# Two transformer layers with expert routing on one core: the passes of the last stage in another order, its row scatters in other groups, its last sums on two engines

## The chip, the core and the metric
One of the cores of a Trainium2 chip runs the whole program. The metric is the device time in microseconds (us); lower is better. The engines are TensorE (PE), VectorE (DVE), ScalarE (ACT), GpSimd (POOL) and SyncE (SP), which mostly issues DMAs. Each works through its own list of instructions in order and waits on semaphores.

## The reference
Input x is 2 x 512 x 256, float32. Four sublayers follow one another, each on the layernorm of x and added to x:
```
x = x + attn0(ln(x))   # delta rule over 512 steps, 16 heads of 16
x = x + ffn0(ln(x))    # 8 experts, top 2, and a shared expert
x = x + attn1(ln(x))   # 16 query heads of 128, 2 key/value heads, causal, softcap 30
x = x + ffn1(ln(x))    # 16 experts, top 6, hidden 176
# ffn1, T = 1024 tokens:
scores = softmax(h @ gate_w.T);  topk_w, topk_idx = top_k(scores, 6)
for e in range(16):
    out = (silu(h @ w_gate[e].T) * (h @ w_up[e].T)) @ w_down[e].T
    y = y + cw[:, e:e+1] * out
```
The change touches the end of attn1 and all of ffn1.

## The kernel before
**attn1** runs over 32 heads n (two batches of 16). Per head TensorE does scores, turns the output of the head before, the next head's queries, the projection of the head before, and the products of probabilities and values; ScalarE does tanh and exp, GpSimd the causal mask (L1138), VectorE the rotations and the normalising.

**ffn1** works on two halves of 512 tokens. For each half the router (`route_a`, `route_b1` to `b3`, VectorE) picks six experts a token, `places1` (TensorE) counts rows, `rows1_index` (VectorE) makes the indices, and GpSimd scatters each row with `send_rows` into a DRAM tensor `rows1`, ordered by expert in blocks of 64 rows: 24 indirect DMAs a half. For the first half (batch 0) this lies in heads 20 to 30: four scatters a head in heads 25 to 30. For the second half it lies in the loop over pairs.

**The loop over pairs** (L1387 TensorE, L1507 ScalarE, L1679 VectorE, L1142 GpSimd) has 64 turns J, 32 a half. A pair is two blocks of 64 rows with possibly two experts. Its steps:
- SP loads its 128 rows (`load_rows`, five buffers).
- turn (`pair_turn`, L657): two transposes of 128 x 128 on TensorE; ScalarE copies the result (`pair_x`).
- gate-up (`pair_gate_up`, L673): the two blocks use the 64-column halves of the array, each with its own expert's weights. The second block's weights are at a place that a register gives; ScalarE copies them to a fixed place first (`pair_copy_gu`, L716), VectorE does the same for down (`pair_copy_dn`, L725).
- silu (ScalarE, L741), mul (VectorE, L754).
- hidden (`pair_hidden`, L685): two transposes of 128 x 88; VectorE copies the result (`pair_h`, L760, here "h").
- down (`pair_down`, L699): 88 x 64 weights, again two halves; ScalarE copies (`pair_y`, L747) into one of 18 buffers, and GpSimd scatters that to DRAM (`send_back`, L781) into a tensor `ret` in token order.

All orders are written out by hand, with the step's number as the condition. In turn J TensorE does turn(J+2), gate-up(J+1), hidden(J), down(J-1), and VectorE mul(J+1), h(J), table copy(J) and then whatever else is set for that J. There is one bank of PSUM each for the results of turn, hidden and down, and two for gate-up. The extras on VectorE: first index back at 1, residual of the last head and layernorm at 2 to 4, the router of the second half at 6 to 11, its index at 12, tables at 13 to 16, and from turn 52 two weighted adds a turn for the first half.

When all of a half's returns have landed, SP loads six tensors of 512 KB (`load_back`, one for each of the six choices, four token tiles each), and VectorE adds tile by tile with the weight as a scalar (`add_back`, L790): 24 adds a half. Then the output is stored.

## Time and profile before
| | us |
|---|---|
| median of 3 runs | 867.38 (866.95 to 867.87) |
| the profiled execution | 867.91 |
| its span, first to last instruction | 866.1 |

| busy, share of the span | |
|---|---|
| TensorE matmul | 789.5 us, 91% |
| VectorE | 507.1 us, 59% |
| ScalarE | 400.1 us, 46% |
| GpSimd | 278.8 us, 32% |
| mean granted TensorE clock | 0.970 |

The profile follows one execution. A start is counted from the span's start. Matmuls are pipelined and their ends are modelled, so lengths are best read from one start to the next. The chain that ended last lies on TensorE for 62% of the span and on VectorE for 12%. The loop over pairs fills the time from 625 to 846 us.

### The profile page before, as it was taken

Reading aid. Unit: us, or ns where it says so; the run is one execution under the profiler, and the core shown is the slowest. Engines: PE = TensorE matmul, PEld = TensorE weight load, DVE = VectorE, ACT = ScalarE, POOL = GpSimd, SP = SyncE. Lnnn points to the kernel's source line nnn. Section 1 sums busy time; section 2 is a strip of 40 time slices with the busy share of each in tenths; the row PEclk is TensorE's granted clock in tenths of the full one; section 3 lists DMA queues with packets and bytes.
Section 4 is the critical chain, followed back from the end, with each engine's and each line's share of the span. In section 5 each row is a group of like instructions: output and inputs, shape, how many; then the busy total and the mean of one; then the engine's idle time right before and its main releaser. Section 6 shows DMA issues by size and latency. Waiting matters only on the chain.

```text
span 866.1 us, 15945 instructions
## 1 busy us (share of the span) xinstructions
PE 789.5 (91%) x5107; PEld 521.6 (60%) x5107; DVE 507.1 (59%) x1270; ACT 400.1 (46%) x856; POOL 278.8 (32%) x374
## 2 busy tenths in 40 slices
PE   5988799889979998999999999899899999999990
PEld 3566566676557785777777767667654444444440
DVE  5999876666512236756556655777534763443564
ACT  3987777555123333443233342232527454555540
POOL 3643744113500033111111111137602265554430
PEclk9998999999989999999999999999979999999995
DMA  4002770181253221044453533113232243537316
GB/s 140 2 1 37 244 257 2 35 238 51 80 165 109 86 67 56 19 142 134 134 159 122 171 92 78 53 50 101 90 68 68 62 126 116 135 117 245 101 46 212
DMA packets 103590, 91.22 MB, mean 105 GB/s; under 512 B 38104, under 2 KB 95448, under 8 KB 103512
## 3 DMA queue, kind: packets, MB, share of 16 engines
q1 hardware_dynamic: 93288, 67.92, 27.2%
q0 software_dynamic: 6912, 19.28, 6.4%
q10 hardware_dynamic: 3312, 3.02, 1.0%
q8 instruction: 45, 0.74, 0.4%
q14 instruction: 33, 0.27, 0.1%
HBM read 50.47 MB, written 38.67 MB: 103 GB/s over the span
## 4 chain that ended last, share of the span: by engine, by line
PE 62%; DVE 12%; issue 6%; POOL 5%; DMA 4%; ACT 3%; DVEq 0%; ACTq 0%; SPq 0%; POOLq 0%
PE bank L1383 8%; PE bank L1346 7%; PE bank L673 7%; PE bank L1240 6%; PE bank L1226 5%; PE bank L699 5%; PE bank L896 3%; PE bank L2166 3%; POOL rows L771 3%; PE bank L918 2%; PE bank L657 2%; PE bank L2123 2%; PE bank L2150 2%; DMA rows<-arena,sidx 2%; PE bank L685 2%
## 5 line engine op out<-in xcount | busy, mean ns | idle before, releaser
L1487 ACT ACTIVATE arena<-bank 128x512 f32<-128x512 f32 (+1 forms) x96 | 46.9, 525 | 147.5 <-PE bank L1346 147.4
L1138 POOL TENSOR_TENSOR arena<-arena,causal_t 128x256 f32<-128x256 f32 x64 | 45.1, 726 | 214.0 <-ACT arena L1492 214.0
L781 POOL DMA_INDIRECT ret<-arena,ridx x64 | 66.1, 1033 | 103.9 <-ACT arena L747 49.9
L673 PE MATMUL bank<-arena 128*64 (+1 forms) x512 | 91.0, 477 | 1.0 <-DVE arena L733 1.0
L1383 PEld LDWEIGHTS bank<-arena 128*128 128x128 f32 x640 | 76.6, 192 | 5.2 <-POOL arena L1138 2.7
L1383 PE MATMUL bank<-arena 128*128 128x129 f32 x640 | 77.5, 276 | 1.7 <-POOL arena L1138 1.7
L1346 PE MATMUL bank<-arena 128*128 128x512 f32 (+3 forms) x256 | 75.7, 440 | 1.4 <-DVE arena L1546 1.4
L699 PE MATMUL bank<-arena 88*64 (+1 forms) x512 | 69.8, 393 | 3.2 <-DVE arena L725 1.7
L754 DVE TENSOR_TENSOR arena<-arena,bank 128x176 f32<-128x176 f32 x64 | 21.6, 337 | 86.2 <-ACT arena L741 86.0
L1240 PE MATMUL bank<-arena 128*128 128x256 f32 x256 | 62.6, 389 | 1.5 <-DVE arena L1553 1.5
L1240 PEld LDWEIGHTS bank<-arena 128*128 128x128 f32 x256 | 49.4, 194 | 22.6 <-issue 12.1
L1226 PE MATMUL bank<-arena 128*128 128x512 f32 x128 | 60.5, 595 | 0.5 <-DVE arena L1544 0.5
L771 POOL DMA_INDIRECT rows<-arena,sidx x48 | 49.9, 1039 | 32.1 <-issue 11.9
L716 ACT COPY arena<-arena 128x704 f32 x64 | 49.7, 778 | 20.5 <-issue 17.1
L1346 PEld LDWEIGHTS bank<-arena 128*128 128x128 f32 x256 | 41.8, 193 | 27.3 <-issue 19.1
L747 ACT COPY arena<-bank 128x256 f32<-128x256 f32 x64 | 23.8, 372 | 69.9 <-PE bank L699 59.8
L673 PEld LDWEIGHTS bank<-arena 128*64 128x64 f32 x512 | 31.5, 137 | 31.8 <-issue 31.6
L1553 DVE COPY arena<-bank 128x256 f32<-128x256 f32 x64 | 24.1, 418 | 42.1 <-PE bank L1250 41.9
L699 PEld LDWEIGHTS bank<-arena 88*64 88x64 f32 x512 | 31.2, 136 | 25.0 <-issue 15.9
L1542 DVE TENSOR_TENSOR arena<-bank,arena 64x512 f32<-64x512 f32 x36 | 24.9, 693 | 35.8 <-PE bank L1226 30.1
L2166 PE MATMUL bank<-w,arena 128*128 128x128 f32 x248 | 35.5, 286 | 7.1 <-DVE w L2699 3.3
L1492 ACT ACTIVATE arena<-arena 128x1280 f32<-128x1280 f32 x32 | 40.6, 1270 | 1.0
(288 smaller groups left out, 1527.0 us busy)
## 6 DMA issues: line engine op xcount, KB each, us to landing
rows<-arena SPq DMA_DIRECT2D x16, 544.0 KB, 4.6
rows_in<-place SPq DMA_DIRECT2D x5, 1664.0 KB, 14.4
arena<-rows SPq DMA_DIRECT2D x64, 128.0 KB, 2.1
arena<-in_w_gu SPq DMA_DIRECT2D x24, 256.0 KB, 3.5
arena<-ret SPq DMA_DIRECT2D x12, 512.0 KB, 6.7
arena<-in_w_dn SPq DMA_DIRECT2D x24, 176.0 KB
arena<-in_wq SPq DMA_DIRECT2D x32, 128.0 KB, 3.9
arena<-in_wo SPq DMA_DIRECT2D x32, 128.0 KB, 2.0
```

Of the source, the lines that this page charges most:

```text
L673: mm = nc.tensor.matmul(p_gu[J % 2][u * HR:(u + 1) * HR, 0:2 * FE].rearrange("p (y n) -> p y n", y=2), pxT[:, J % 2, k, u * HR:(u + 1) * H ...
L699: mm = nc.tensor.matmul(p_y[u * HR:(u + 1) * HR, :], phT[0:HB, J % 2, q, u * HR:(u + 1) * HR], w[u][:, q, :], start=(q == 0), stop=(q == 1 ...
L716: nc.scalar.copy(wbg[:, J % 2, :], w1_gu[:, bass.ds(off, GU1)]).then_inc(s_wbg, 1)
L771: nc.gpsimd.indirect_dma_start(rows1[h], bass.IndirectOffsetOnAxis(ap=sidx1[:, h, i % K1, i // K1:i // K1 + 1], axis=0), xa[h][:, i // K1, ...
L781: nc.gpsimd.indirect_dma_start(ret[h], bass.IndirectOffsetOnAxis(ap=ridx[:, h, j:j + 1], axis=0), py[J % NY], None).then_inc(s_ret, 16)
L1138: nc.gpsimd.tensor_tensor(blocks, blocks, causal_t[:].unsqueeze(1).to_broadcast([P, 2, P]), ALU.mult).then_inc(s_p, 1)
L1226: mm = nc.tensor.matmul(b_q[:], wq[:, n % 2, k, :], xnT2[:, k, b * SEQ:(b + 1) * SEQ], start=(k == 0), stop=(k == KD - 1))
L1240: mm = nc.tensor.matmul(b_y[t // 2][:, (t % 2) * DIM:(t % 2 + 1) * DIM], oT[:, t * P:(t + 1) * P], wo[:, n % 2, :], start=first and t % 2 ...
L1346: mm = nc.tensor.matmul(b_s[sbank][:, o:o + w], kT[:, grp, kt * P:(kt + 1) * P], qr[:, kt * P:SEQ], start=True, stop=True, skip_group_chec ...
L1383: mm = nc.tensor.matmul(b_o[pair][:, t * (DH + 1):(t + 1) * (DH + 1)], pr[:, o:o + P], v[:, grp, kt, :], start=(kt == 0), stop=(kt == qb))
L1487: nc.scalar.activation(th[:, sbank * 512:sbank * 512 + w], b_s[sbank][:, 0:w], ACT.Tanh, scale=SCALE / SOFTCAP).then_inc(s_th, 1)
L2166: mm = nc.tensor.matmul(sacc[h][:, j * P:(j + 1) * P], kq[:, u, hq * P:(hq + 1) * P], ub[s][:, hq, :], start=False, stop=True, skip_group_ ...
```

## The change
TensorE's order in turn J becomes turn(J+2), hidden(J-1), gate-up(J+1), down(J-1); the first gate-up comes behind head 31's values. VectorE's order becomes h(J-1), mul(J+1), table copy(J). The extras get other turns: first index back 4 (from 1), both stats 2, normalise 3, router 5, 6, 8, 10, index 11, tables 13, 15, 16, 17, three adds a turn in 54 to 61. The first half's scatters go in groups of five in heads 25 to 29, the second half's in four groups of six. The second half's returns are loaded from two queues (SP and ScalarE); token tiles 0 and 1 are added on VectorE, tiles 2 and 3 by TensorE with diagonal matrices of the weights, which VectorE writes in turns 40 to 45, and one add from PSUM. Scatter groups wait for the group before, as they did. On TensorE the extras of turn J stand behind hidden(J-1) and ahead of gate-up(J+1); before they stood behind down(J-1): the turn of head 31 at 0 (now 1), its projection at 1 (now 2), the layernorm's turns at 5 (now 4), logits at 6 (now 5), places at 12 (now 11).
```diff
+    dg = at(14600, 2 * K1 * P).rearrange("p (i n) -> p i n", n=P)
...
-        def send_rows(self, pool, h, groups):
+        def send_rows(self, pool, h, lo, hi):
...
+            if lo == 0:
...
+            else:
+                pool.wait_ge(s_rows, SC + SC1 * h + 16 * lo)
+            for i in range(lo, hi):
...
+        def spread_weights(self, dve, k):
+            if k == 0:
+                dve.wait_ge(s_rows, SC + 2 * SC1)
+            for t in (2, 3):
+                ins = nc.vector.scalar_tensor_tensor(out=dg[:, 2 * k + t - 2, :], in0=ident[:], scalar=wk1[:, 1, k, t:t + 1],
+                                                     in1=ident[:], op0=ALU.mult, op1=ALU.mult)
+            if k == K1 - 1:
+                ins.then_inc(s_rx1, 1)
+        def sum_back(self, pe):
+            pe.wait_ge(s_rx1, 3)
+            for k in range(K1):
+                pe.wait_ge(s_ys[k], ys_0[k] + 32)
+                for t in (2, 3):
+                    mm = nc.tensor.matmul(b_y[0][:, (t - 2) * DIM:(t - 1) * DIM], dg[:, 2 * k + t - 2, :], ys[k][:, t, :],
+                                          start=(k == 0 and t == 2), stop=(k == K1 - 1), skip_group_check=True)
+            mm.then_inc(s_y, 1)
...
-                if J == NP1 + 18:
-                    self.load_back(sp, 0)
+                if J == NP1 + 16:
+                    self.load_back(sp, 0, range(K1))
-            self.load_back(sp, 1)
+            self.load_back(sp, 1, range(0, K1, 2))
-                sp.wait_ge(s_xres.sem, 18 + 2 * q)
+                sp.wait_ge(s_xres.sem, 18 + q)
...
-                if 25 <= n < 31:
-                    self.send_rows(pool, 0, (n - 25,))
+                if 25 <= n < 30:
+                    self.send_rows(pool, 0, 5 * (n - 25), min(5 * (n - 24), 4 * K1))
-                    self.send_rows(pool, 1, range(K1))
+                    for t in range(4):
+                        self.send_rows(pool, 1, t * K1, (t + 1) * K1)
...
-                    self.pair_gate_up(pe, 0, offs[0])
+            self.pair_gate_up(pe, 0, offs[0])
             for J in range(2 * NP1):
                 if J + 2 < 2 * NP1:
                     self.pair_turn(pe, J + 2)
+                if J:
+                    self.pair_hidden(pe, J - 1)
+                if J == 4:
+                    pe.wait_ge(s_xres.sem, 12)
+                    self.ln_turn(pe, 10)
+                    self.ln_turn(pe, 11)
+                if J == 1:
+                    self.turn(pe, NH - 1)
+                if J == 5:
+                    self.logits(pe, 3)
+                if J == 11:
+                    self.places1(pe, 1)
+                if J == 2:
+                    self.project(pe, NH - 1)
                 if J + 1 < 2 * NP1:
                     self.pair_gate_up(pe, J + 1, offs[J + 1])
                 if J + 3 < 2 * NP1:
                     offs.append(owners(J + 3))
-                self.pair_hidden(pe, J)
                 if J:
                     self.pair_down(pe, J - 1, offs[J - 1])
-                if J == 0:
-                    self.turn(pe, NH - 1)
-                if J == 1:
-                    self.project(pe, NH - 1)
...
+            self.pair_hidden(pe, 2 * NP1 - 1)
             self.pair_down(pe, 2 * NP1 - 1, offs[2 * NP1 - 1])
+            self.sum_back(pe)
...
-                if J == 3:
+                if J == 2:
                     self.ln_std(act, 10)
                     self.ln_std(act, 11)
-                if J == 5:
+                if J == 4:
                     self.ln_evac(act, 10)
                     self.ln_evac(act, 11)
-                if J == 6:
+                if J == 5:
                     self.exps(act, 3)
             self.pair_y(act, 2 * NP1 - 1)
+            act.wait_ge(s_xres.sem, 16)
+            self.load_back(act, 1, range(1, K1, 2))
...
+            self.pair_mul(dve, 0)
             for J in range(2 * NP1):
+                if J:
+                    self.pair_h(dve, J - 1)
+                if J == 1:
+                    self.turned(dve, NH - 1)
                 if J + 1 < 2 * NP1:
                     self.pair_mul(dve, J + 1)
-                self.pair_h(dve, J)
                 self.pair_copy_dn(dve, J)
...
-                if NP1 + 20 <= J < 2 * NP1:
-                    for i in range(2 * (J - NP1 - 20), 2 * (J - NP1 - 19)):
+                if NP1 + 8 <= J < NP1 + 8 + K1:
+                    self.spread_weights(dve, J - NP1 - 8)
+                if NP1 + 22 <= J < NP1 + 30:
+                    for i in range(3 * (J - NP1 - 22), 3 * (J - NP1 - 21)):
                         self.add_back(dve, 0, i)
+            self.pair_h(dve, 2 * NP1 - 1)
             for i in range(4 * K1):
-                self.add_back(dve, 1, i)
+                if i % 4 < 2:
+                    self.add_back(dve, 1, i)
+            dve.wait_ge(s_y, NH + 1)
+            self.residual(dve, 6, b_y[0])
```

## Rows read from the trace of the kernel before

**Rows 1.** Stretches: us; busy us (count) PE PEld DVE ACT POOL; clock, DMA share, GB/s.
```profile
556.00:560.00 4.00, 1.54 (x14) 1.38 (x14) 2.72 (x8) 0.00 (x0) 0.00 (x0) 1.00 0.41 125
561.90:565.30 3.40, 3.40 (x11) 2.52 (x10) 0.52 (x2) 2.16 (x4) 0.00 (x0) 0.52 0.00 0
627.80:636.80 9.00, 7.95 (x24) 4.96 (x25) 1.19 (x3) 0.44 (x2) 0.00 (x0) 0.50 0.59 106
785.00:805.00 20.00, 20.00 (x134) 8.66 (x132) 6.85 (x21) 11.72 (x27) 7.85 (x8) 1.00 0.74 252
851.00:859.00 8.00, 0.00 (x0) 0.00 (x0) 5.66 (x14) 0.00 (x0) 0.00 (x0) 0.50 1.06 359
```

**Rows 2.** TensorE in order of time, last pairs: start, us, engine, line, what.
```profile
835.28 1.08 PE L699 MATMUL bank<-arena 88*64 x8
836.29 0.44 PE L657 MATMUL bank<-ident,arena 128*128 128x128 f32 x2
836.66 1.40 PE L673 MATMUL bank<-arena 128*64 x8
838.00 0.42 PE L685 MATMUL bank<-ident,arena 128*88 128x128 f32 x2
838.34 1.08 PE L699 MATMUL bank<-arena 88*64 x8
839.26 1.35 PE L673 MATMUL bank<-arena 128*64 x8
840.54 0.42 PE L685 MATMUL bank<-ident,arena 128*88 128x128 f32 x2
```

**Rows 3.** TensorE in order of time, head of the loop; idle before in brackets.
```profile
627.81 0.69 PE L657 MATMUL bank<-ident,arena 128*128 128x128 f32 x2 [3.26 <-DMA arena<-rows]
628.29 3.62 PE L1240 MATMUL bank<-arena 128*128 128x256 f32 x8
...
633.38 2.62 PE L673 MATMUL bank<-arena 128*64 x8 [1.04 <-DVE arena L733]
```

**Rows 4.** GpSimd in order of time: last scatter of the first half.
```profile
623.30 0.96 POOL L771 DMA_INDIRECT rows<-arena,sidx  x1 [0.30 <-issue]
```

**Rows 5.** VectorE in order of time: the last sums.
```profile
853.03 10.56 DVE L790 SCALAR_TENSOR_TENSOR x_sb<-arena,wk,x_sb 128x256 f32<-128x256 f32 x24 [8.17 <-DMA arena<-ret]
```

**Rows 6.** TensorE in order of time: passes of one width in a row.
```profile
640.34 0.42 PE L685 MATMUL bank<-ident,arena 128*88 128x128 f32 x2
640.60 0.60 PE L1250 MATMUL bank<-ident,arena 128*128 128x128 f32 x4
641.03 0.38 PE L657 MATMUL bank<-ident,arena 128*128 128x128 f32 x2
641.35 1.40 PE L673 MATMUL bank<-arena 128*64 x8
```

**Rows 7.** Groups by line from 600 us: busy us, mean ns; idle before, releaser.
```profile
L725 DVE COPY arena<-arena 88x512 f32 x64 | 28.5, 445 | 14.0 <-issue 9.0 <-PE bank L699 4.9
...
L760 DVE COPY arena<-bank 88x256 f32<-88x256 f32 x64 | 26.4, 413 | 0.2 <-PE bank L685 0.2
...
L741 ACT ACTIVATE arena<-bank 128x176 f32<-128x176 f32 x64 | 20.4, 319 | 13.8 <-PE bank L673 13.2
```

**Rows 8.** TensorE in order of time: two waits in the loop.
```profile
674.72 0.39 PE L685 MATMUL bank<-ident,arena 128*88 128x128 f32 x2 [0.94 <-DVE arena L760]
...
736.38 1.08 PE L699 MATMUL bank<-arena 88*64 x8 [0.83 <-issue]
```

**Rows 9.** Stretches of VectorE extras: us, VectorE busy (count), clock, DMA share, GB/s.
```profile
649.33:651.67 2.34, 2.27 (x8) 1.00 0.36 110
...
670.67:673.87 3.20, 3.06 (x6) 1.00 0.24 71
...
686.95:691.09 4.14, 3.83 (x17) 1.00 0.12 32
```

**Rows 10.** ScalarE in order of time: a table load in the loop.
```profile
667.85 1.28 ACT L741 ACT_TABLE_LOAD   x1
```

More of the change, by code:

```diff
@@ L760, in pair_h @@
             nc.vector.tensor_copy(phT[0:HB, J % 2, :, :], p_h[0:HB, :].rearrange("p (q n) -> p q n", q=2)).then_inc(s_pte, 1)
-        def send_rows(self, pool, h, groups):
-            for g in groups:
-                if g == 0:
-                    pool.wait_ge(s_pl, DI1[h])
-                    pool.wait_ge(ln_xn, NT + 20 + 4 * h)
-                    pool.wait_ge(s_zf, ZF1)
-                else:
-                    pool.wait_ge(s_rows, SC + SC1 * h + 64 * g)
-                for i in range(4 * g, 4 * g + 4):
-                    nc.gpsimd.indirect_dma_start(rows1[h], bass.IndirectOffsetOnAxis(ap=sidx1[:, h, i % K1, i // K1:i // K1 + 1], axis=0),
-                                                 xa[h][:, i // K1, :], None).then_inc(s_rows, 16)
+        def send_rows(self, pool, h, lo, hi):
+            if lo == 0:
+                pool.wait_ge(s_pl, DI1[h])
+                pool.wait_ge(ln_xn, NT + 20 + 4 * h)
+                pool.wait_ge(s_zf, ZF1)
+            else:
+                pool.wait_ge(s_rows, SC + SC1 * h + 16 * lo)
+            for i in range(lo, hi):
+                nc.gpsimd.indirect_dma_start(rows1[h], bass.IndirectOffsetOnAxis(ap=sidx1[:, h, i % K1, i // K1:i // K1 + 1], axis=0),
+                                             xa[h][:, i // K1, :], None).then_inc(s_rows, 16)
         def send_back(self, pool, J):
@@ L1008, in load_rows, with load_back @@
             sp.dma_start(xr[:, J % NW, :], rows1[h][j * P:(j + 1) * P, 0:DIM]).then_inc(s_xl[J % NW], 16)
-        def load_back(self, sp, h):
-            sp.wait_ge(s_ret, RE0 + 16 * (h + 1) * NP1)
-            for k in range(K1):
-                sp.dma_start(ys[k], ret[h][1 + k * HALF:1 + (k + 1) * HALF, :].rearrange("(t p) d -> p t d", p=P)).then_inc(s_ys[k], 16)
+        def load_back(self, eng, h, ks):
+            eng.wait_ge(s_ret, RE0 + 16 * (h + 1) * NP1)
+            for k in ks:
+                eng.dma_start(ys[k], ret[h][1 + k * HALF:1 + (k + 1) * HALF, :].rearrange("(t p) d -> p t d", p=P)).then_inc(s_ys[k], 16)
         def sp(self, sp, attn0):
@@ L1080, in sp @@
                 self.load_rows(sp, J)
-                if J % NP1 == 1:
+                if J in (1, NP1 + 1):
                     h = J // NP1
@@ L1368, in pe @@
                     self.pair_turn(pe, 0)
+                if n == NH - 2:
+                    offs = [owners(J) for J in range(3)]
                 if n:
@@ L1374, in pe @@
                     self.pair_turn(pe, 1)
-                    offs = [owners(J) for J in range(3)]
-                    self.pair_gate_up(pe, 0, offs[0])
                 pe.wait_ge(s_p, n * 2 + 2)
@@ L1637, in dve @@
                     self.pair_x(dve, 1)
-                    self.pair_mul(dve, 0)
                 for pair in range(2):
@@ L1691, in dve @@
                     self.residual(dve, 6, b_y[1])
+                if J == 2:
                     self.ln_stats(dve, 10)
+                    self.ln_stats(dve, 11)
                 if J == 3:
-                    self.ln_stats(dve, 11)
-                if J == 4:
                     self.ln_norm(dve, 10)
                     self.ln_norm(dve, 11)
+                if J == 5:
+                    self.route_a(dve, 3)
                 if J == 6:
-                    self.route_a(dve, 3)
-                if J == 7:
                     self.route_b1(dve, 3)
-                if J == 9:
+                if J == 8:
                     self.route_b2(dve, 3)
+                if J == 10:
+                    self.route_b3(dve, 3)
                 if J == 11:
-                    self.route_b3(dve, 3)
-                if J == 12:
                     self.rows1_read(dve, 1)
```

21 lines of the change are left out of this document (6 added, 15 removed).

## The prediction

> **What bounds the kernel now.** Four views, in this order. First the stretches: in the second half of the last stage TensorE is busy all the time and VectorE about a third of it [rows 1], so there TensorE's own length per pair is the bound. Then TensorE in order of time: a pair takes 3.06 to 3.07 us, made of down 1.01, turn 0.37, gate-up 1.34 and hidden 0.34, each counted from one start to the next [rows 2]. Then the start of the loop, where TensorE waits 3.26 us for the last row scatter [rows 3, 4]. Last the tail: all matmuls are done, six loads arrive, and 24 adds on VectorE take 10.56 us [rows 5].
>
> **The basis.** The profiled execution took 867.91 us, its span is 866.1; the median of the runs is 867.38. I work the sum on the first and take off the 0.5 us that the median lies below it.
>
> **Part 1, the order of the passes.** Today each pair goes turn (128 wide), gate-up (64), hidden (128), down (64): four changes. New: turn, hidden, gate-up, down: two. What a change costs is seen where two passes of one width happen to meet. Where down is followed by a gate-up, it takes 0.92 instead of 1.01, and that gate-up takes 1.28 instead of 1.34 [rows 2]: 0.16 together. Where a hidden and a turn have 128-wide neighbours, hidden takes 0.26 (not 0.34) and the turn 0.32 (not 0.37) [rows 6]: 0.13. Sum 0.29 a pair, so 2.78 instead of 3.07. The trace shows neither boundary in the direction that the new loop uses (turn then hidden, gate-up then down). Bounds: both save nothing (0), both save in full (0.29); only the 128-wide one saves (0.13). I take 0.29, the nearest rows. For 62 pairs: **-18.0 us** (lower end -8, and 0).
> The Trainium skill (TensorEngine Tiling (Array Packing), Key Properties) says that a change of tiling mode drains the engine and that a change of tile alone does not. Gate-up and down are both 64 wide with more than 64 rows, one mode, so by it the pair saves in full in either direction; by the 128-wide boundary alone the term would be -8. No row shows the new direction.
>
> **Part 2, the head of the loop.** The last of 24 scatters of the first half is issued at 623.30 [rows 4], in head 30; TensorE waits 3.26 us for the rows. Its clock then drops: 0.50 (1.2 of 2.4 GHz) over 627.8 to 636.8 [rows 1], so that a projection takes 3.42 us from its start to the turn behind it, twice what it takes at full clock, and the first gate-up 2.55 instead of 1.34, after another 1.04 us idle [rows 3]. New: groups of five, so the last scatter goes out in head 29, one head of 8.3 us sooner, and its rows are there. GpSimd then has some 1.6 us of masks and five scatters of about 1.3 (0.96 and the issue behind it [rows 4]) in a head: 8.1 of 8.3 us, which just fits; up to 0.5 us late is a bound I take as 0. TensorE's order by hand from 624.4: turn 0.3, wait for the copies of head 30 0.65, projection 1.73, turn 0.3, wait for the last mask 0.25, values 2.25, gate-up 1.24, turn 0.3, gate-up 1.24, a wait of 0.4 for ScalarE's copy: turn 3 starts at 633.1, not 641.03: **-7.9 us** (bounds -5 and -8.5).
>
> **Part 3, what stands before the copy of hidden.** This speaks against the change. Down(J) needs VectorE's copy h(J). VectorE now does, in turn J: h(J-1), mul(J+1), table copy(J), then the extras of J (layernorm, router, tables, adds), and only then h(J). Count from the end of gate-up(J+1): silu 0.12 + 0.32, mul 0.29 (its start to the next), table copy 0.52 with its issue, extras X, h 0.41, back to TensorE 0.15 [rows 7]: 1.81 + X. TensorE's own work in between is 2.78. So only **X up to 0.97 us** is free; the rest idles TensorE. After a stall the next turn has that much more room. Before, h(J) was needed a whole pair later, and an extra of 3.20 us cost 0.94 us of waiting, and 0.3 behind it [rows 8, 9]. Stretches of extras in the trace (seven, three shown [rows 9]): residual and first stats 2.34 and second stats 1.02, normalise 1.78, router 3.20, 2.47, 1.73, index 4.14. New stalls, by turn:
> J=2, 3.36 in one turn: 2.4. J=3 and 4: the square root waits for those stats, then copy, copy, an activation table of 1.28 [rows 10], silu, mul, table copy, normalise 1.78: 6.2 us from the end of the stats, in which TensorE has 2.1 of work left, so 0.4 and 3.6. J=5: logits wait for the evacuation, 1.1. J=6: two more table loads hold silu 7, then router 3.20: 0.7 and 4.3. J=8: 1.5. J=11: places wait for the router's last part, 1.6; index 4.14: 3.2. J=13, 15, 16, 17 and 34 (1.7, 1.4, 1.6, 1.4, 1.86 us): 0.7, 0.4, 0.2, 0.2, 0.9. J=54 to 61, three adds of 0.44 instead of two: 0.33 every second turn, 1.3. After the last gate-up nothing stands between hidden and down: 1.6. The weights' diagonals (two of about 0.3 us in six turns) are under 0.97: 0. Sum **+24.1**. The stalls of the same places that go: 3.9 us between turns 3 and 17 (the 0.94 of [rows 8] is the longest) and 1.1 at the end: **-5.0**. A further hidden falls behind turn 3: **+0.4**. Bounds for the new stalls: 14 (if ScalarE's tables overlap more than I see) and 28.
>
> **Part 4, the clock in those stalls.** An idle time of 2.46 us at 557 (busy 1.54 of 4 us) was followed by a stretch of 3.4 us at half clock, and the 3.26 us one by 9 us of it [rows 1]. I expect four idle times of 2.4 us or more; half clock for 3.4 us takes 1.7 us of work, part of it where VectorE is the bound anyway. Three drops of 1.7: **+5** (bounds 0 and 4 x 3.5 = 14, the 3.5 being what part 2's stretch lost).
>
> **Part 5, GpSimd.** Today copies for pairs 26 on wait for return slots, since 24 scatters in six groups hold GpSimd; TensorE idles 0.83 us once, 1.7 with the two waits that follow [rows 8]. New: four groups, two waits of some 2 us less, and pair 26 comes 45 us behind the first scatter (42 before), needed at 41: **-1.7** (bound 0). The first return sends begin later (index at turn 4) but have 30 us for ten of 1.27: 0. The loads of the first half's returns start two pairs sooner; rows behind them have 6 pairs of 2.78 = 16.7 us and need 14: 0.
>
> **Part 6, the tail.** Last return landed at 849.2, first load 853.0, the adds end at 863.6 [rows 5]. New: VectorE adds half (12 x 0.44), TensorE the other half as 12 weighted matmuls of 256 columns, then one residual of 0.68. The DMA engines are full from 851 to 859 at 359 GB/s [rows 1], so two queues bring the first two tensors together at 854.4 and the last at 859.5 as before. TensorE is at half clock there: 0.855 each by the slow projection [rows 3], 10.3 us from 854.4, plus 0.8: 865.5, **+1.9**. At full clock the last four take 1.7: 862.1, **-1.5**. I take **0**: it starts slow and may rise.
> The Trainium skill (Trainium Kernel Development and Optimization, Key Constraints) says that queues of several engines share the same 16 DMA engines and save only issue time. The trace agrees as far as it goes, with the engines' share at 1.06; by a doubled rate the part would have been about -4, by the rule it is the 0 above.
>
> **Sum.** -18.0 - 7.9 + 24.1 - 5.0 + 0.4 + 5 - 1.7 + 0 = -3.1: 864.8 for the profiled kind, **864.3** as a median.
>
> **Rivals.**
> A, the clock holds, or the stalls are shorter. Speaks for it: behind the 0.94 us at 674.7 it held [rows 8]. Then the 5 us go, and perhaps 3 of stalls: 867.4 - 8 to - 11 = 859.4 to 856.4. Against it: 2.46 us was enough at 557 [rows 1].
> B, slower: the clock falls at each long stall of turns 2 to 11 and stays down as at the head, 3.5 us a time, four times 14 instead of 5. Place: 640 to 695 us. It decides as soon as the clock takes more than 8.1 us. Time 867.4 - 8.1 + 14 = 873.3. For it: 9 us of half clock behind one wait [rows 1]. Against: after 557 it lasted 3.4.
> C, the 64-wide boundary (gate-up to down, 128 to 88 rows) saves nothing: part 1 gives -8, the slower TensorE hides 2.5 us more of stalls: 864.3 + 10 - 2.5 = 871.8. Against it: the same two widths the other way saved 0.16.
> D, the tail at half clock throughout: +1.9, 866.2, within what counts as no change. 0.2% (1.7 us) is about what a measurement of this kernel can tell from none.
>
> **How the numbers follow.** Forecast (861 to 867) 0.42, A 0.26, B 0.12, C 0.10, D 0.10. Faster by more than 0.2% (under 865.6): A whole, three quarters of the forecast: 0.57. Within 0.2%: the rest of the forecast below 869 and D: 0.20. Slower: B, C: 0.23. Range 855 to 873; the forecast's own is 861 to 867.
>
> **What would show it.** The pair's period in turns 20 to 33: 2.78 right, 2.94 is C, 3.07 no effect. Turn 3's start near 633 with no half clock before it. TensorE idle ahead of down, releaser VectorE's h copy, about 4 us at turn 7, 3 at turn 12, and at 4 ahead of the layernorm turn; if these are under 1 us the rule of 0.97 is wrong. Granted clock 0.5 in three stretches of 640 to 700. In the tail, matmuls of 0.85 us and a residual that ends last. The prediction fails if extras turn out to be hidden, or if the clock lies low for tens of us.

## The result, and the profile after

| | kernel before | changed kernel |
|---|---|---|
| median | 867.62 us (866.95 to 869.79, 4 runs) | 876.87 us (875.85 to 878.74, 4 runs) |
| profiled execution, span | 867.91, 866.1 | 876.53, 874.7 |
| mean granted TensorE clock | 0.970 | 0.962 |

The ratio is 1.0105 (95%: 1.008 to 1.013): 9 us slower, where 3 us faster was forecast. The same two kernels, measured again on two chips (B and E below), gave 1.0119 (1.0068 to 1.0169) and 1.0116 (1.0087 to 1.0144).

The span splits at four points that both traces have: the start of the turn with index 3 (turn(3), which TensorE does in turn 1), of those with indices 22 and 63, and the end of the last down. The forecast's terms are sorted the same way.

| stretch, us | before | after | difference | forecast |
|---|---|---|---|---|
| start to turn(3) | 641.03 | 632.76 | -8.3 | -7.9 |
| turn(3) to turn(22) | 67.86 | 91.92 | +24.1 | +16.3, of it 5 for the clock |
| turn(22) to turn(63) | 127.40 | 119.05 | -8.4 | -11.4 |
| turn(63) to the end of down | 9.77 | 11.65 | +1.9 | -0.1 with the next line |
| the tail | 20.0 | 19.4 | -0.7 | |
| sum | | | +8.6 | -3.1 |

Of the first line's 8.3 us, 1.3 lie ahead of 560 us, where the two programs are alike: the wait of 2.46 us in the heads ends at 559.57 before and at 558.23 after, and from there to turn(3) it is 81.46 against 74.52, so the change itself gives 6.9. The loss lies in the second line. First what went as forecast. TensorE of the changed kernel in order of time (start, length, engine, line, what), two pairs in the middle of the loop; L701 is down, L659 turn, L687 hidden, L675 gate-up:

```profile
737.65 1.04 PE L701 MATMUL bank<-arena 88*64 x8
738.62 0.44 PE L659 MATMUL bank<-ident,arena 128*128 128x128 f32 x2
738.89 0.38 PE L687 MATMUL bank<-ident,arena 128*88 128x128 f32 x2
739.21 1.40 PE L675 MATMUL bank<-arena 128*64 x8
740.44 1.03 PE L701 MATMUL bank<-arena 88*64 x8
```

From down to down it takes 2.79 us, where the old order took 3.07 [rows 2]; gate-up to down is 1.23 and turn to hidden 0.27, so both new boundaries save in full. The Trainium skill (TensorEngine Tiling (Array Packing), Key Properties) says that a change of tiling mode drains the engine and a change of tile alone does not; the trace agrees, with 3.07 us a pair for four changes of width and 2.79 for two.

The head of the loop, the same view:

```profile
632.76 0.41 PE L659 MATMUL bank<-ident,arena 128*128 128x128 f32 x2 [0.18 <-ACT arena L737]
633.00 0.38 PE L687 MATMUL bank<-ident,arena 128*88 128x128 f32 x2
```

turn(3) starts at 632.76 (forecast 633.1), without the wait of 3.26 us and the half clock behind it [rows 3].

Now the loss. Stretches of the changed kernel (us; busy us and count of PE, PEld, DVE, ACT, POOL; granted clock, DMA share, GB/s):

```profile
640.00:655.00 15.00, 10.44 (x52) 5.34 (x50) 6.86 (x22) 6.43 (x12) 0.00 (x0) 0.67 0.08 19
655.00:670.00 15.00, 14.13 (x70) 7.91 (x66) 4.73 (x14) 7.76 (x15) 4.84 (x5) 0.64 0.19 61
670.00:685.00 15.00, 11.43 (x68) 5.32 (x68) 9.44 (x18) 5.64 (x13) 3.35 (x4) 0.89 0.17 54
685.00:700.00 15.00, 9.99 (x62) 5.38 (x58) 8.38 (x27) 4.39 (x11) 2.67 (x3) 0.88 0.14 45
700.00:740.00 40.00, 37.10 (x252) 18.63 (x252) 19.60 (x53) 21.77 (x50) 26.55 (x26) 0.96 0.41 131
740.00:780.00 40.00, 38.77 (x280) 20.04 (x276) 17.31 (x46) 23.82 (x56) 22.14 (x23) 1.00 0.45 126
```

A mean of 0.67 over 15 us means 2 x 0.33 x 15 = 9.9 us at 0.50 (1.2 GHz). The five upper rows give 9.9 + 10.8 + 3.3 + 3.6 + 3.2 = 30.8 us at half clock (30.7 by the clock's record, in five pieces: two of 10.2 us from 645.2 and 658.9, three of 3.4 us from 676.0, 689.6 and 699.8). The kernel before has 1.00 in all of them. VectorE is busy a third to two thirds of the time in each of them, so it is not short of time: TensorE waits for it at fixed places. What TensorE waits for between turn(3) and turn(22) (engine, line <- releaser: us in total, times, longest):

```profile
PE bank L701 <- DVE arena L762: 12.2, 7, 3.2
PE bank L489 <- DVE arena L479: 2.1, 1, 2.1
PE bank L577 <- DVE arena L569: 1.8, 1, 1.8
```

Down waits seven times for the copy h (L762); the two other rows are the layernorm's turns and places. One of the seven, from the same kernel: TensorE at the stall and behind it.

```profile
674.03 1.08 PE L701 MATMUL bank<-arena 88*64 x8 [2.55 <-DVE arena L762]
675.05 0.44 PE L659 MATMUL bank<-ident,arena 128*128 128x128 f32 x2
675.32 0.38 PE L687 MATMUL bank<-ident,arena 128*88 128x128 f32 x2
675.64 2.35 PE L675 MATMUL bank<-arena 128*64 x8
```

The gate-up that starts 1.6 us behind the wait of 2.55 takes 2.35 instead of 1.40: the clock has fallen. The fall at 658.9 has no such wait close before it. The stretch ahead of it, the logits' wait in it, and the stretch at half clock:

```profile
655.50:658.80 3.30, 2.44 (x22) 1.72 (x18) 2.64 (x7) 2.42 (x6) 0.00 (x0) 1.00 0.15 40
657.74 2.58 PE L512 MATMUL bank<-rw,xnT 128*128 128x16 f32 x16 [0.86 <-ACT xnT L502]
658.90:669.10 10.20, 10.20 (x42) 5.42 (x43) 1.56 (x6) 4.73 (x8) 4.81 (x5) 0.50 0.23 77
```

So a wait of 0.86 stood ahead of a fall here, where 0.94 in the kernel before had none behind it [rows 8].

The tail (SP and ScalarE issue, VectorE and TensorE sum):

```profile
858.49 1.47 SPq L1032 DMA_DIRECT2D arena<-ret  x3
858.55 1.53 ACTq L1032 DMA_DIRECT2D arena<-ret  x3
863.25 1.87 DVE L809 SCALAR_TENSOR_TENSOR x_sb<-arena,wk,x_sb 128x256 f32<-128x256 f32 x4 [9.98 <-DMA arena<-ret]
...
869.50 1.99 PE L799 MATMUL bank<-arena 128*128 128x256 f32 x8 [0.61 <-DMA arena<-ret]
...
871.53 0.69 DVE L1562 TENSOR_TENSOR x_sb<-x_sb,bank 128x512 f32<-128x512 f32 x1 [0.19 <-PE bank L799]
```

The loads come in pairs 3 us apart and set the end; TensorE's share is 12 products, and the last four (two records each) take 1.99 us, and one add of 0.69 follows, against 10.56 us of adds before [rows 5].

### The profile page after: what moved, and what is told of

Read it like the earlier page. It is cut to its first block, busy times and chain, and to the rows that moved or that the text cites. A ratio compares the mean times of both kernels' runs of the same rounds, so it can differ in the third digit from the quotient of the medians.

```text
span 874.7 us, 15992 instructions
## 1 busy us (share of the span) xinstructions
PE 793.2 (91%) x5131; PEld 536.4 (61%) x5131; DVE 506.9 (58%) x1271; ACT 400.8 (46%) x856; POOL 278.6 (32%) x374
## 4 chain that ended last, share of the span: by engine, by line
PE 67%; DVE 14%; ACT 7%; issue 6%; DMA 3%; POOL 2%; DVEq 0%; SPq 0%; ACTq 0%; POOLq 0%
PE bank L675 8%; PE bank L1403 8%; PE bank L1366 7%; PE bank L1260 6%; PE bank L701 6%; PE bank L1246 5%; PE bank L915 3%; PE bank L2199 3%; PE bank L937 2%; PE bank L659 2%; ACT arena L2256 2%; PE bank L2156 2%; PE bank L2183 2%; DVE sh L2737 1%; PE bank L1270 1%
## 5 line engine op out<-in xcount | busy, mean ns | idle before, releaser
L1157 POOL TENSOR_TENSOR arena<-arena,causal_t 128x256 f32<-128x256 f32 x64 | 45.1, 726 | 215.0 <-ACT arena L1516 214.9
L675 PE MATMUL bank<-arena 128*64 (+1 forms) x512 | 96.6, 501 | 0.0
L701 PE MATMUL bank<-arena 88*64 (+1 forms) x512 | 71.8, 403 | 17.8 <-DVE arena L762 17.2
L701 PEld LDWEIGHTS bank<-arena 88*64 88x64 f32 x512 | 36.9, 145 | 55.8 <-issue 46.8
L756 DVE TENSOR_TENSOR arena<-arena,bank 128x176 f32<-128x176 f32 x64 | 21.5, 336 | 74.5 <-ACT arena L743 74.2
L1260 PEld LDWEIGHTS bank<-arena 128*128 128x128 f32 x256 | 48.1, 190 | 23.6 <-issue 12.7
L1366 PEld LDWEIGHTS bank<-arena 128*128 128x128 f32 x256 | 42.0, 194 | 27.6 <-issue 19.4
L675 PEld LDWEIGHTS bank<-arena 128*64 128x64 f32 x512 | 32.7, 143 | 33.8 <-issue 33.6
L1579 DVE COPY arena<-bank 128x256 f32<-128x256 f32 x64 | 24.1, 418 | 42.4 <-PE bank L1270 42.2
L727 DVE COPY arena<-arena 88x512 f32 x64 | 28.2, 441 | 28.1 <-PE bank L701 21.6
```

The lines of the kernel that those rows point to most:

```text
L675: mm = nc.tensor.matmul(p_gu[J % 2][u * HR:(u + 1) * HR, 0:2 * FE].rearrange("p (y n) -> p y n", y=2), pxT[:, J % 2, k, u * HR:(u + 1) * H ...
L701: mm = nc.tensor.matmul(p_y[u * HR:(u + 1) * HR, :], phT[0:HB, J % 2, q, u * HR:(u + 1) * HR], w[u][:, q, :], start=(q == 0), stop=(q == 1 ...
L1157: nc.gpsimd.tensor_tensor(blocks, blocks, causal_t[:].unsqueeze(1).to_broadcast([P, 2, P]), ALU.mult).then_inc(s_p, 1)
L1260: mm = nc.tensor.matmul(b_y[t // 2][:, (t % 2) * DIM:(t % 2 + 1) * DIM], oT[:, t * P:(t + 1) * P], wo[:, n % 2, :], start=first and t % 2 ...
L1366: mm = nc.tensor.matmul(b_s[sbank][:, o:o + w], kT[:, grp, kt * P:(kt + 1) * P], qr[:, kt * P:SEQ], start=True, stop=True, skip_group_chec ...
```

## Experiments

The runs lie on five chips (A to E). On B, D and E the kernel before takes 866.7 to 868.5 us. On A and C it takes 877 to 878, and there the variants that were traced lose another 16 to 24 us between turn(16) and turn(32). Each chip was used at one time only, so a chip and a passing state of it can't be told apart here. So every ratio is to the kernel before on the same chip, and what the variants say of the change is read from turn(3) to turn(16) (ahead of that loss) and from turn(32) to turn(63) (behind it). The stretches are those of the profiled execution; for mul first (874.4) and threes (852.3) it took 6 us more than the median, and the 6 us lie ahead of turn(3).

| kernel | chip | us | ratio (95%) | (3) to (16) | (16) to (32) | (32) to (63) |
|---|---|---|---|---|---|---|
| before, traced again | B | 867.5 | 1.001 (0.999-1.003) | 48.7 | 53.3 | 95.1 |
| before, traced again | D | 868.4 | 1.000 (0.997-1.003) | 48.7 | 51.4 | 95.1 |
| changed | B | 876.6 | 1.012 (1.007-1.017) | 71.7 | 48.1 | 90.6 |
| changed | E | 877.0 | 1.012 (1.009-1.014) | 72.0 | 48.1 | 91.1 |
| changed, filler | E | 867.9 | 1.001 (0.999-1.003) | 63.2 | 48.1 | 90.9 |
| changed, filler | A | 887.1 | 1.012 (1.008-1.015) | 63.2 | 66.9 | 91.4 |
| changed, filler | C | 887.7 | 1.012 (1.009-1.015) | 63.8 | 67.4 | 91.2 |
| mul first | C | 867.6 | 0.989 (0.987-0.992) | 48.8 | 68.6 | 87.1 |
| split only | C | 890.5 | 1.015 (1.012-1.019) | 65.5 | 69.0 | 90.9 |
| extras behind h | A | 885.0 | 1.012 (1.005-1.019) | 64.3 | 64.5 | 87.9 |
| old order, sixes | A | 876.2 | 0.999 (0.997-1.001) | 48.8 | 66.6 | 95.4 |
| old order, fours | B | 858.6 | 0.990 (0.985-0.994) | 48.7 | 50.5 | 95.1 |
| spread, sixes | A | 868.5 | 0.990 (0.986-0.994) | 48.0 | 68.6 | 87.8 |
| spread, sixes | C | 867.3 | 0.989 (0.986-0.992) | 48.0 | 68.2 | 87.1 |
| spread, sixes | D | 843.4 | 0.972 (0.968-0.977) | 47.9 | 44.7 | 86.4 |
| spread, fours | B | 845.1 | 0.976 (0.971-0.981) | 47.9 | 45.2 | 86.6 |
| spread, fours | D | 842.5 | 0.971 (0.967-0.975) | 47.9 | 45.1 | 86.4 |
| spread, threes | D | 846.3 | 0.974 (0.970-0.978) | 47.9 | 47.3 | 86.6 |

Where an expectation says nothing of the chip, its numbers are for one where the kernel before takes 867.

### What the half clock costs

The changed kernel with products of the identity in the long stalls, ahead of the instruction that waits:

```diff
+        def filler(self, pe, n, bk):
+            for _ in range(n):
+                nc.tensor.matmul(bk[:, 2 * P:3 * P], ident[:], ident[:], start=True, stop=True, skip_group_check=True)
 ...
+                if J in (3, 7, 9, 12):
+                    self.filler(pe, {3: 10, 7: 16, 9: 5, 12: 13}[J], bank[1] if J < 12 else bank[7])
                 if J:
                     self.pair_down(pe, J - 1, offs[J - 1])
```

(14, 4 and 6 more ahead of the layernorm turn, logits and places.)

Chip A: 

> The changed kernel with filler matmuls (identity by identity, about 0.21 us each, results unused) ahead of seven TensorE instructions that wait: 10, 14, 4, 16, 5, 6, 13 of them in turns 3, 4, 5, 7, 9, 11, 12. They add work and take no wait away. Theory (the half clock behind the stalls costs 8 to 14 us): granted clock 1.0 through 640 to 705, 863 to 869 us. Rival (half clock costs nothing since VectorE is the bound there): 876 to 879 us, or more by the filler.

Chip C: 

> The changed kernel with filler products in its long stalls, once more, on a chip without the loss in turns 21 to 32. Theory clock: the half clock costs the changed kernel 8 us or more in turns 3 to 22; with it held they take 83 to 85 us instead of 91.9, no stretch under 1.00, and the ratio to the kernel before is 0.999 to 1.003 instead of 1.011. Rival stalls: the stalls end no sooner (VectorE sets them), so what the clock gives is waited for again; turns 3 to 22 take 88 us or more, ratio 1.006 or more.

Chip E, beside the changed kernel: 

> The changed kernel beside its variant with filler products, on one chip. If the kernel before takes 867 here: 876.7, ratio 1.011. If it takes 877: theory (the loss in turns 18 to 32 falls on it as on the others) 892 to 896, ratio 1.017 to 1.021, with periods of 4 us and more in turns 18 to 32; rival (the changed kernel is spared) 882 to 886, ratio under 1.010.

> The changed kernel with TensorE kept busy by filler products in its long stalls. Theory clock: half clock costs the changed kernel 7 to 9 us in turns 3 to 17; with it held, this one is 6 to 9 us faster than the changed kernel on the same chip (868 to 871 where the kernel before takes 867). Rival stalls: VectorE sets the ends of the stalls, so the clock given back is waited for: within 3 us of the changed kernel.

On E the filler variant takes 867.86 us, the changed kernel 877.03: 9.2 us, of which 8.7 lie between turn(3) and turn(22) (83.47 against 92.20), all ahead of turn(16). Stretches of the filler variant on E:

```profile
640.00:655.00 15.00, 14.48 (x112) 9.98 (x109) 7.25 (x24) 6.85 (x14) 0.00 (x0) 1.00 0.07 19
655.00:670.00 15.00, 14.05 (x110) 10.14 (x110) 8.19 (x20) 8.39 (x17) 5.81 (x6) 1.00 0.25 80
670.00:685.00 15.00, 14.07 (x106) 8.93 (x106) 8.16 (x17) 6.61 (x15) 4.84 (x4) 1.00 0.23 72
685.00:700.00 15.00, 13.58 (x101) 8.13 (x102) 9.61 (x35) 5.54 (x13) 5.85 (x6) 1.00 0.22 74
```

The clock is 1.00 throughout. Theory clock holds, rival stalls falls: the changed kernel has 30.7 us at half clock on E too, and they cost 9 us. The fillers can only add time of their own, so 9 us is the least that the half clock costs. The ratios of 1.012 on A and C were misses, and so were the 83 to 85 us for turn(3) to turn(22) (89.7 and 93.1), by the loss of those two chips; the turns ahead of it (63.2, 63.8) agree with E. The changed kernel itself was expected as it came on E.

### What the stalls without the clock are made of

With the clock held, turn(3) to turn(22) still takes 83.47, 15.6 more than before, where the forecast without its clock term has 11.3. VectorE, TensorE and ScalarE of the filler variant on E around one extra (two router steps, L554 and L555):

```profile
672.76 1.03 PE L705 MATMUL bank<-arena 88*64 x8
672.97 0.32 ACT L747 ACTIVATE arena<-bank 128x176 f32<-128x176 f32 x1 [0.24 <-PE bank L679]
673.32 0.34 DVE L760 TENSOR_TENSOR arena<-arena,bank 128x176 f32<-128x176 f32 x1 [1.27 <-ACT arena L747]
...
674.06 0.42 DVE L731 COPY arena<-arena 88x512 f32 x1 [0.41 <-PE bank L705]
...
674.41 1.21 DVE L554 TENSOR_TENSOR arena<-arena,tri 128x1024 f32<-128x1024 f32 x1
...
675.65 1.23 DVE L555 TENSOR_TENSOR arena<-arena 128x1024 f32<-128x1024 f32 x1
...
676.91 0.42 DVE L766 COPY arena<-bank 88x256 f32<-88x256 f32 x1
...
677.48 1.08 PE L705 MATMUL bank<-arena 88*64 x8 [0.46 <-DVE arena L766]
```

Gate-up ends where down starts, at 672.76. Silu starts 0.21 later, mul 0.35 after it, the table copy 0.74 after mul, the extra 0.35 after that: 1.65. The extra is 2.50 (674.41 to 676.91), and down follows the start of h by 0.57. So the chain is 2.22 + X, not 1.81 + X, and in a pair of 2.79 the free room is 0.57 us, not 0.97. The missing 0.4 is for the most part 0.28 in mul and table copy (1.09 together, 0.41 of it idle ahead of the copy, where the forecast had 0.81) and 0.1 ahead of silu. In the kernel before that idle time is 9.0 + 4.9 us over 64 copies, 0.22 each [rows 7]; in the changed kernel the same group has it doubled (releasers last):

```profile
L727 DVE COPY arena<-arena 88x512 f32 x64 | 28.2, 441 | 28.1 <-PE bank L701 21.6
```

The profile names down as the releaser, but by the kernel table copy(J) waits only for down(J-2), which had ended 3 us earlier; mul first has 0.16 to 0.32 there in most turns. What the 0.41 is made of stays open.

Three kernels tell the room from the length of the extras. "Mul first" is the changed kernel with

```diff
                 if J:
+                    self.pair_mul(dve, J)
                     self.pair_h(dve, J - 1)
 ...
-                if J + 1 < 2 * NP1:
-                    self.pair_mul(dve, J + 1)
                 self.pair_copy_dn(dve, J)
```

> The changed kernel with one thing moved: in a turn of VectorE mul(J) comes ahead of h(J-1), instead of mul(J+1) behind it; the extras stay where they are. An extra then needn't wait for the gate-up that TensorE is at, and from one copy h to the next stand 0.34 + 0.41 + 0.5 us and the extra in a pair of 2.78. Theory room: extras up to some 2.0 us are free instead of 0.97; each of about 12 stalls is 1.1 us shorter and two stretches of half clock fall away: 20 us less in turns 3 to 22 at best, 12 at least; 857 to 865, ratio 0.989 to 0.997. Rival length: what counts is the long extras (3.2 and 4.1 us), and one place or the other changes little: 870 or more, ratio over 1.003.

"Split only" keeps the changed order of VectorE and halves the long extras (router, index) over more turns. It also puts layernorm, logits and places behind down on TensorE, moves the extras by up to two turns, the first index back to 0, and starts the second half's scatters at 12 instead of 10. The router's part of it:

```diff
-                if J == 6:
-                    self.route_b1(dve, 3)
                 if J == 8:
-                    self.route_b2(dve, 3)
+                    self.route_b1(dve, 3, 0)
+                if J == 9:
+                    self.route_b1(dve, 3, 1)
+                    self.route_b2(dve, 3, 0)
                 if J == 10:
-                    self.route_b3(dve, 3)
+                    self.route_b2(dve, 3, 1)
+                    self.route_b3(dve, 3, 0)
                 if J == 11:
+                    self.route_b3(dve, 3, 1)
```

> The fourth experiment's split extras (2.4 us at most, router and index over twice as many turns, layernorm, logits and places behind down) but mul(J+1) behind h(J-1) as in the changed kernel. Theory room: every split extra still exceeds 0.97 us, by 0.5 to 1.4 in some 13 turns, 12 to 14 us of stalls, none long enough to bring the clock down; turns 3 to 22 take 72 to 78 us, 857 to 862, ratio 0.989 to 0.994. Rival length: with the long ones split the stalls are gone, turns 3 to 22 take 66 us, ratio 0.976 to 0.982.

"Extras behind h" puts extras(J-1) between h(J-1) and mul(J+1), so that they delay mul and not h:

```diff
-                self.pair_copy_dn(dve, J)
+            def extras(J):
                 if J == 4:
                     self.rows1_back(dve, 0)
 ...
+            for J in range(2 * NP1):
+                if J:
+                    self.pair_h(dve, J - 1)
+                    extras(J - 1)
 ...
+                if J + 1 < 2 * NP1:
+                    self.pair_mul(dve, J + 1)
+                self.pair_copy_dn(dve, J)
```

> The changed kernel with the extras of a turn moved by two places in VectorE's list: h(J), extras(J), mul(J+2), table copy(J+1), instead of extras(J) ahead of h(J). Same instructions, same turns. Theory (extras ahead of h have 0.97 us of room, behind it 2.17): each long stall shrinks by some 1.2 us, the adds of turns 54 to 61 stall no more, fewer clock drops, 857 to 866 us. Rival (VectorE's amount of work in these turns counts, not its place): 875 to 878 us.

Turn(3) to turn(16): changed 71.7, extras behind h 64.3, split only 65.5, mul first 48.8. One moved line brings back 22.9 us: 14.4 of them against the filler variant's 63.2, which has the clock held, and 8.5 by the clock. Splitting alone brings 6.2 at most, since half of its index falls behind turn(16). VectorE of mul first, with the same router steps of 3.20 us that cost the changed kernel 2.55 (L756 mul, L762 h, L701 down):

```profile
663.86 1.23 DVE L547 TENSOR_TENSOR arena<-arena 128x1024 f32<-128x1024 f32 x1
...
665.12 1.23 DVE L548 TENSOR_TENSOR arena<-arena 128x1024 f32<-128x1024 f32 x1
...
666.38 0.34 DVE L756 TENSOR_TENSOR arena<-arena,bank 128x176 f32<-128x176 f32 x1
...
666.63 0.41 DVE L762 COPY arena<-bank 88x256 f32<-88x256 f32 x1
667.19 1.08 PE L701 MATMUL bank<-arena 88*64 x8 [1.17 <-DVE arena L762]
```

The extra no longer begins behind gate-up, silu, mul and table copy of its own turn; it starts at 663.15, while TensorE is in down, and 3.20 cost 1.17: room 2.0. Theory room holds on the turns; its times of 857 to 865 were missed on chip C, where the kernel before has 878, but the ratio of 0.989 is the expected one. For split only both sides were wrong: the theory expected no half clock and 12 to 14 us of stalls, the rival no stalls. It has stalls up to 3.2 us (13.2 us in six waits up to 706 us), because a table load of ScalarE, which delays silu and mul, adds to a short extra, and the clock was down in parts (mean 0.93, 0.89, 0.77 and 0.89 in the four stretches from 640 to 700). One of 2.88, in its trace:

```profile
652.95 1.28 ACT L761 ACT_TABLE_LOAD   x1
...
654.24 0.32 ACT L761 ACTIVATE arena<-bank 128x176 f32<-128x176 f32 x1
...
654.59 0.34 DVE L774 TENSOR_TENSOR arena<-arena,bank 128x176 f32<-128x176 f32 x1 [3.76 <-ACT arena L761]
...
657.36 0.41 DVE L780 COPY arena<-bank 88x256 f32<-88x256 f32 x1
...
657.91 1.08 PE L719 MATMUL bank<-arena 88*64 x8 [2.88 <-DVE arena L780]
```

Extras behind h freed the adds of the last turns (87.9 instead of 91.2 behind turn(32)) and shortened the waits for h ahead of 700 us (3.8 us in two), but not the rest: two waits of 3.4, behind the square root that waits for the stats and at the layernorm's turns, and one of 2.2 at places, with the clock at 0.86 to 0.89 in three of the four stretches. With the 16.4 us that it lost between turn(16) and turn(32) against the changed kernel taken off, 885.0 is 868.6: over the 857 to 866 of the theory and under the 875 to 878 of the rival, so place counts, but here for less than expected.

### Head and tail alone, and the order with room

The old order of passes and extras with the new head and tail, second half's scatters in sixes (chip A), then in fours (chip B):

```diff
-                    for t in range(4):
-                        self.send_rows(pool, 1, t * K1, (t + 1) * K1)
+                    for t in range(K1):
+                        self.send_rows(pool, 1, 4 * t, 4 * t + 4)
```

> The changed kernel with one part undone: TensorE's and VectorE's order in the loop over pairs and the turns of the extras are those of before; the new head, scatter groups, load queues and last sums stay. Theory (the extras ahead of the copy of hidden, and the clock that falls in the stalls, cost more than the width changes save): turn 3 starts near 633, the pair takes 3.07 us, no half clock between 640 and 700, time 857 to 860 us. Rival (the new head, groups or last sums are what costs): 867 or more.

> The old order of passes and of VectorE's extras with the new head and the new tail, and the second half's scatters in six groups of four as before (in the first experiment they were four groups of six). Theory chip: the groups do not matter for the loss in turns 21 to 32; ratio to the kernel before 0.991 (the 7.9 us of the head, nothing else), which the experiment with groups of six (0.999) did not reach because the chip's loss fell harder on it. Rival groups: with fours the loss goes, 0.988 to 0.991 here, and turns 22 to 63 take 127.4 us; with sixes it would stay. Third: the head's gain is given back later whatever the groups, ratio 0.999.

On B it takes 858.6 against 867.0: head and tail are worth 8.5 us by themselves, and turn(3) to turn(22) has its old 67.8. On A the same parts gave nothing, the 16 us lost between turn(16) and turn(32) having eaten them; as the two runs differ in chip and in groups, they don't tell these apart.

"Spread" is split only, with all that this moves, and mul first on top. In sixes on chip A, then fours on B, then sixes on C:

> The changed kernel with the order mul(J), h(J-1), table copy(J), extras on VectorE (mul one turn later), the router's and the index's long parts split over more turns so that none is over about 2.4 us, TensorE's layernorm turns, logits and places behind down, and 12 instead of 10 returns sent ahead of the second half's scatters. Theory: with at most 2.17 us of extras in a turn the pair keeps its 2.79 us nearly throughout, no half clock, 844 to 851 us. Rival (another engine, ScalarE with its table loads or GpSimd with the returns, becomes the bound at 2.79): 855 or more, with waits on ScalarE or on the return slots.

> The two-width order with VectorE's extras split to 2.4 us at most and mul(J) and the copy h(J-1) at the head of the turn, as in the fourth experiment (0.990 of the kernel before), but the second half's scatters in groups of four. Theory chip: same as with groups of six, ratio 0.985 to 0.992. Rival groups: 10 us less than with sixes, ratio 0.975 to 0.980.

> The fourth experiment once more (scatters of the second half in four groups of six). With six groups of four on another chip the same kernel came to 0.976 of the kernel before; with sixes on the earlier chip to 0.990. Theory chip: on a chip where the kernel before takes about 867, this one takes 845, ratio 0.973 to 0.980, and turns 22 to 63 take 115 us. Rival groups: 855 to 858, ratio 0.986 to 0.990, with periods of 4 us and more in turns 21 to 32.

A and C gave 0.990 and 0.989, B 0.976, which is the number that the rival groups had; the run on C told nothing between them, since that chip has the loss too. So the three group sizes were run on D, beside the kernel before:

> The spread order with four scatter groups of six. Theory queue (what runs while more scatters are out is held until the group has landed): more is lost with sixes than with fours on the same chip, 867 against 855 if the kernel before takes 877. Rival chip: sixes and fours take the same to 2 us; 845 where the kernel before takes 867, 855 where it takes 877.

> The same kernel with six groups of four; it took 845.1 us where the kernel before took 867.0. Theory queue: ratio 0.972 to 0.978 on any chip, and at least 8 us less than with sixes. Rival chip: within 2 us of the sixes; ratio 0.972 to 0.978.

> The same kernel with eight groups of three: four more waits of about 1.5 us on GpSimd than with fours ends the scatters 3 to 6 us later. Theory queue: what is lost in turns 18 to 32 falls further, but late return slots (pair 26 and on) give back 2 to 4: between 2 us under and 4 us over the fours. Rival chip: no loss to win, so 2 to 5 us over the fours from the late slots.

On D sixes take 843.35 and fours 842.53: no difference that these runs can tell. The groups of six in the change cost nothing there, and the gap between A and B was the chip's: the same sixes give 0.972 on D. Threes add 3.8 us, as expected from late slots: one wait of 2.2 us for rows is 2.3 of it between turn(16) and turn(32). Spread with fours or sixes is the best version: with fours 0.9709 (0.9671 to 0.9748), 26 us under the kernel before and some 34 under the changed one of the other chips. Most of it is mul first: on chip C that alone takes 867.57 and spread 867.32. Mul first wasn't run on a chip without the loss, so whether the split is worth anything there isn't shown. What TensorE waits for in it (sixes, D) from turn(3) to 700 us:

```profile
PE bank L719 <- DVE arena L780: 3.6, 6, 0.8
PE bank L677 <- ACT arena L755: 1.0, 3, 0.5
```

No wait is longer than 0.8 us, and the clock is 1.00 from 640 to 740.

### The loss on two chips

> The kernel before, unchanged, for its profile beside the others on one chip. On the chip of the last four runs it took 876.9 us instead of 867.6, and the four kernels there all lost 10 to 14 us in turns 21 to 32, where the second half's scatters run. Theory chip: that loss belongs to the chip. Then, if this chip takes about 877 for this kernel, its turns 21 to 32 show periods of 4 to 10 us instead of 3.07 and turns 22 to 63 take some 137 us instead of 127.4. Rival groups: the loss comes from scatter groups of six; then this kernel, with its groups of four, shows 127.4 there and any difference in its time lies elsewhere. If the chip is like the first one: 867.6 and 127.4.

> The changed kernel, unchanged, on the same chip as the others of this call. Theory (the clock is the term that was too small, the rest as forecast): ratio to the kernel before 1.010, turns 3 to 22 take 92 us with 25 to 35 us at half clock, whatever the chip adds to both. Rival: the 9 us came from the state of one chip; then the ratio here is under 1.000.

> The kernel before, for its profile beside the next three. If this chip takes 877 for it: theory (loss of the chip while scatters are out) turns 18 to 32 show periods of 4 us and more and turns 22 to 63 take 134 to 138 us; rival (the whole kernel is slower there): every pair 3.10 instead of 3.07 and the attention heads longer than 8.95 us a head. If it takes 867: 127 to 129 us, as on the first chip.

Neither trace of the kernel before fell on such a chip (127 to 129 us from turn(22) to turn(63), as on the first). So the loss is shown for the variants alone; that the kernel before has part of it follows only from its 877 us. One such place, spread with sixes on C (L790 is a row scatter, L767 ScalarE's copy of down):

```profile
709.34 0.37 ACT L767 COPY arena<-bank 128x256 f32<-128x256 f32 x1 [4.10 <-remote]
709.38 0.32 SPq L1045 DMA_DIRECT2D arena<-rows  x1
709.43 0.42 DVE L780 COPY arena<-bank 88x256 f32<-88x256 f32 x1 [3.82 <-remote]
709.67 1.04 POOL L790 DMA_INDIRECT rows<-arena,sidx  x1 [1.74 <-DMA rows<-arena,sidx]
709.99 1.53 PE L719 MATMUL bank<-arena 88*64 x6 [2.99 <-DVE arena L780]
```

ScalarE, SP, VectorE and GpSimd all go on within 0.33 us, at the moment when the six scatters have landed. What holds them isn't in the trace. The same stretch on D has TensorE busy all the time. All eight kernels traced on A and C had sixes, and the longest such idle time of VectorE was 7.9 us. Whether fours would lose less than sixes on such a chip wasn't tried.

## Why the prediction was wrong, step by step

**Part 1, the order of the passes: right.** Forecast 2.78 a pair, measured 2.79. Rival C (2.94) falls.

**Part 2, the head: right.** -8.3 against -7.9, or 6.9 from the point up to which the programs are alike; head and tail together, without the rest, 8.5.

**Part 3, what stands before the copy of hidden: the mechanism right, the room mis-sized. This is the step that failed by most.** The sum's "1.81 + X" is 2.22 + X, the free room 0.57 instead of 0.97. I took mul and the table copy as 0.81 together where they take 1.09. Some ten stalls are longer, by 0.4 each if the room alone counts: 15.6 us without the clock where 11.3 were forecast, +4.3. Read off the filler variant as a turn's time over 2.79: 4.6 at J = 7 (4.3 forecast), 3.5 for the index (3.2), and 1.5, 1.0 and 1.1 for the tables of J = 13, of 15, of 16 and 17 (0.7, 0.4, 0.4). Behind turn(22) it is the same error: the stall of J = 34 is 1.46 instead of 0.9, the three adds cost 0.64 and 0.19 every second turn instead of 0.33 (2.5 in all instead of 1.3), and 0.8 comes from a few turns that had 1.0 to 1.3 us of extras and were taken as free, the weights' diagonals among them: +3.0 with rounding. At the end it is 2.0 more up to the last down, of which some 0.9 is the clock (that down takes 1.98 instead of 1.03), and the tail gives 0.7 back: +1.3. The places of the big ones were right.

**Part 4, the clock in the stalls: a term too small, and its condition wrong.** "Three drops of 1.7: +5", with 3.4 us at half clock each, 10 in all. There were five, 30.8 us in all, and they cost 9.2 (filler against changed on one chip; 8.7 in the stretch). I had looked for a drop behind each wait of 2.4 us or more; between 640 and 700 there were three such waits (2.48, 2.55, 3.20), and two of the drops had only 0.86 and 1.81 us close ahead of them. The length was three times the forecast. The price per us at half clock was lower than I counted (0.3 instead of 0.5), since the waits for VectorE hide a part: from turn(8) to turn(10) the changed kernel, partly at half clock, takes 10.5 us, and the filler variant at full clock 10.5 as well. This is rival B, to which I gave 0.12: its place (640 to 695 us) is met, and its condition (more than 8.1 us) narrowly. Its 14 us are not. The forecast took the short drop behind 557 for the rule and the long one at the head [rows 1] for the exception. Here waits of 0.9 us and more follow each other at 5 to 16 us, and between two drops the clock is back for 3.4 to 10.2 us.

**Part 5, GpSimd: right.** The waits at 736 [rows 8] are gone (1.7 us), and nothing took their place; the groups of six cost nothing beside fours on D.

**Part 6, the tail: right, a little better.** -0.7 against 0. Rival D (+1.9) falls. The Trainium skill (Trainium Kernel Development and Optimization, Key Constraints) says that two queues share the same DMA engines; the trace agrees: from the first issue to the last landing the six loads take 11.3 us from two queues and took 11.0 from one.

**The misses together:** head -0.4 (without the 1.3 us ahead of it, +1.0); turn(3) to turn(22) +7.8, of it 4.3 the room and 3.5 to 4.2 the clock (by difference, and by the two kernels' times); to turn(63) +3.0; the end +1.3. That is the 11.7 us between +8.6 and -3.1. With all but the clock right the forecast would have been 873.0, with the clock alone right 868.3 (both for the profiled execution, 876.5): the two errors are needed together.

## What to carry to other kernels

When a reordering turns a slack consumer into a chain across three engines, count the chain from start to start in the trace, with the idle time ahead of each instruction in steady state; a group's mean idle hides it. Put what is long behind all the steps that TensorE needs next, and not ahead of or between two of them (extras behind h, between h and mul, gained little): here the place of one multiplication was worth 23 us (8.5 of them by the clock) and the splitting of the long extras at most 6. A train of stalls is a risk for the clock that one stall's price doesn't show: here, with 17 us of waits in 92 us, TensorE ran at half clock for 31 us, which cost 9. And compare variants on one chip, in stretches.

## What the runs showed that I had not expected

- Filler products in the stalls of a TensorE that only waits are worth 9.2 us (877.03 to 867.86 on one chip), with no other change.
- On two of five chips something holds ScalarE, VectorE and SP for 2 to 8 us at a time while groups of row scatters are out (in the place shown, until the group has landed), and costs the variants 16 to 24 us between turn(16) and turn(32). It isn't explained here.
